# The last layer of 24 chunks as three reduced-precision products per tile in place of one full-precision product

## The reference

```
x = layernorm(x + relu((adj @ x) @ kernel + bias))
u, v = x, v_node_feats
for _ in range(3):
    v = mlp_uv(adj @ u)      # three 128x128 layers, each followed by leaky_relu
    u = mlp_vu(adj @ v)
x = layernorm(x + v)
```

## The kernel before

| rows | chunks | loads at offsets from 12 on |
|---|---|---|
| 1 | 4 | 14 (after a copy of a PSUM bank to `part`, L580), 16, 22, 24 |
| 2 to 5, and 6 in the last of the four passes | 17 | 12, 14, 20, 22 |
| 6 in the other three passes | 3 | 16, 18, 24, 26 |

## Time and profile before

### The profile page before, as it was taken

How to read it: one execution, slowest core, us unless ns; L and a number is a source line. 1 busy time by engine, 2 the same in 40 slices (tenths; PEclk the granted TensorE clock), 3 DMA queues, 4 the chain that set the end, 5 groups by cost and what they waited for, 6 DMA issues and landing times.

```text
span 1169.0 us, 13697 instructions
## 1 busy us (share of the span) xinstructions
PE 1154.0 (99%) x5236; PEld 953.1 (82%) x5236; DVE 738.2 (63%) x890; ACT 660.8 (57%) x809; POOL 0.2 (0%) x4
## 2 busy tenths in 40 slices
PE   7999999999999999999999999999999999999997
PEld 6888888888888888888888888888888888887776
DVE  7997676458564555555545756554566555658886
ACT  7765554346554555555444754554566454557885
POOL 0000000000000000000000000000000000000000
PEclk9999999999999999999999999999999999999999
DMA  9988775568466646555656736655665566569891
GB/s 383 405 299 327 244 270 192 206 215 288 124 207 209 215 161 214 198 185 180 216 180 216 250 118 216 214 173 181 210 222 188 190 205 209 193 217 362 296 323 50
DMA packets 72210, 261.60 MB, mean 224 GB/s; under 512 B 8017, under 2 KB 8657, under 8 KB 71121
## 3 DMA queue, kind: packets, MB, share of 16 engines
q1 hardware_dynamic: 72000, 260.61, 64.2%
q10 hardware_dynamic: 144, 0.13, 0.0%
HBM read 258.61 MB, written 2.10 MB: 223 GB/s over the span
## 4 chain that ended last, share of the span: by engine, by line
PE 92%; DMA 3%; DVE 2%; ACT 2%; issue 1%; SPq 0%; DVEq 0%; ACTq 0%
PE agg_ps L872 28%; PE agg_ps L865 28%; PE agg_ps L858 28%; PE pre_ps L769 4%; DMA adj_raw<-in_adj 3%; PE hid_ps L730 1%; PE hid_ps L732 1%; PE hid_ps L731 1%; DVE adj_lo L722 1%; ACT adj_hi L593 1%; PE hid_ps L791 1%; PE hid_ps L805 0%; DVE stats L606 0%; ACT hid L487 0%; ACT resid L508 0%
## 5 line engine op out<-in xcount | busy, mean ns | idle before, releaser
L722 DVE TENSOR_TENSOR adj_lo<-adj_raw,adj_hi 128x1024 fp32r<-128x1024 f32 x488 | 576.7, 1220 | 230.2 <-ACT adj_hi L593 224.0
L858 PE MATMUL agg_ps<-adj_hi,feat_hi 128*128 128x512 f32 x1532 | 607.7, 397 | 7.4 <-ACT adj_hi L593 7.4
L865 PE MATMUL agg_ps<-adj_hi,feat_lo 128*128 128x512 f32 x1532 | 598.0, 390 | 0.0
L593 ACT ACTIVATE adj_hi<-adj_raw 128x1024 fp32r<-128x1024 f32 x488 | 492.8, 1052 | 94.8 <-PE agg_ps L872 80.3
L872 PE MATMUL agg_ps<-adj_lo,feat_hi 128*128 128x512 f32 x1532 | 473.8, 390 | 0.2 <-DVE adj_lo L722 0.2
L858 PEld LDWEIGHTS agg_ps<-adj_hi,feat_hi 128*128 128x128 f32 x1532 | 288.5, 188 | 68.8 <-issue 10.2
L865 PEld LDWEIGHTS agg_ps<-adj_hi,feat_lo 128*128 128x128 f32 x1532 | 288.5, 188 | 62.2 <-issue 3.4
L872 PEld LDWEIGHTS agg_ps<-adj_lo,feat_hi 128*128 128x128 f32 x1532 | 287.8, 188 | 61.9 <-DVE adj_lo L722 1.5
L487 ACT ACTIVATE hid<-hid_ps,params 128x512 f32<-128x512 f32 (+1 forms) x80 | 54.5, 681 | 59.1 <-PE hid_ps L732 50.6
L558 ACT ACTIVATE in_hi<-part 128x512 fp32r<-128x512 f32 x24 | 15.2, 634 | 110.3 <-DVE part L711 110.3
L487 ACT ACTIVATE post<-pre 128x512 f32<-128x512 f32 x39 | 24.6, 630 | 79.8 <-DVE pre L689 79.8
(11 more groups left out here) (70 smaller groups left out, 262.2 us busy)
## 6 DMA issues: line engine op xcount, KB each, us to landing
adj_raw<-in_adj SPq DMA_DIRECT2D x472, 512.0 KB, 5.7
adj_raw<-in_adj SPq DMA_DIRECT2D x8, 1024.0 KB, 8.1
resid<-in_x SPq DMA_DIRECT2D x8, 256.0 KB, 8.0
out<-resid SPq DMA_DIRECT2D x7, 256.0 KB, 6.8
params<-in_weights SPq DMA_DIRECT2D x1, 386.0 KB, 4.7
b_row<-in_bias_rows SPq DMA_DIRECT2D x1, 128.0 KB, 5.5
out<-resid ACTq DMA_DIRECT2D x1, 128.0 KB, 2.1
out<-resid SPq DMA_DIRECT2D x1, 128.0 KB, 2.2
```

Of the source, the lines that this page charges most:

```text
L593: act.activation(adj_hi[:, plan.slot[b], i * CHUNK:(i + pieces) * CHUNK], adj_raw[:, h % RAW, 0:pieces * CHUNK], ACT.Copy).then_inc(adj_hi ...
L722: dve.tensor_tensor(adj_lo[:, plan.slot[b], slot], adj_raw[:, h % RAW, 0:pieces * CHUNK], adj_hi[:, plan.slot[b], slot].bitcast(F32), ALU. ...
L858: pe.matmul(group_bank(g), feat_hi[feats][:, tile(src, i)], adj_hi[:, plan.slot[b], piece(i)], start=start, stop=False)
L865: pe.matmul(group_bank(g), feat_lo[feats][:, tile(src, i)], adj_hi[:, plan.slot[b], piece(i)], start=False, stop=False)
```

## The change

The last layer (`pe_out`) of the 24 `IN_PARTS` chunks is made in parts. For each of its four tiles three F32R products of 128 x 128 take the place of one full-precision product. ScalarE writes the high part `hid2_hi` from PSUM ahead of `hid2`; VectorE writes `hid2_lo` in a new step `dve_hid2=16`; the last layer's two weights are split once, at tick 320. The steps `pe_out`, `dve_pre`, `act_post` and `dve_feat` move one tick later.

```diff
-                   pe_out=18, dve_pre=19, act_post=20, dve_feat=22),
+                   dve_hid2=16, pe_out=19, dve_pre=20, act_post=21, dve_feat=23),
...
+    def out_in_parts(self, u):
+        return "dve_hid2" in STEPS[self.steps_of(u)]
...
                     act.wait_ge(params_loaded, 32)
                     act.activation(w_hi[:, :, :], w_hid, ACT.Copy).then_inc(w_hi_ready, 1)
+                    act.activation(w_out[:, :, 0:P], w_last, ACT.Copy).then_inc(w_out_hi_ready, 1)
...
+                    if plan.out_in_parts(u):
+                        prelu(hid2_hi[:, :], hid2_ps[:, :], bias=b_col[:, b:b + 1]).then_inc(hid2_hi_ready, 1)
                     prelu(hid2[:, own(u)], layer_bank(1, u), bias=b_col[:, b:b + 1]).then_inc(hid2_ready, 1)
...
+                    dve.wait_ge(w_out_hi_ready, 1)
+                    dve.tensor_tensor(w_out[:, :, P:2 * P], w_last, w_out[:, :, 0:P].bitcast(F32), ALU.subtract)\
+                       .then_inc(w_out_lo_ready, 1)
...
+                u = at(t, "dve_hid2", DEEP)
+                if u is not None:
+                    dve.wait_ge(hid2_hi_ready, plan.count_out_in_parts(u))
+                    dve.wait_ge(hid2_ready, u + 1)
+                    dve.tensor_tensor(hid2_lo[:, :], hid2[:, :], hid2_hi[:, :].bitcast(F32), ALU.subtract)\
+                       .then_inc(hid2_lo_ready, 1)
...
-                    for k, j in enumerate(tiles_of(u)):
+                    if plan.out_in_parts(u):
+                        k = SPLIT_OUT[kind_of(u)]
+                        if plan.count_out_in_parts(u) == 1:
+                            pe.wait_ge(w_out_lo_ready, 1)
+                        pe.wait_ge(hid2_lo_ready, plan.count_out_in_parts(u))
+                        for j in tiles_of(u):
+                            nodes = slice(j * P, (j + 1) * P)
+                            last = product(pre_ps[:, nodes], (hid2_hi[:, nodes], hid2_lo[:, nodes]),
+                                           (w_out[:, k, 0:P], w_out[:, k, P:2 * P]))
+                    for k, j in enumerate(tiles_of(u) if not plan.out_in_parts(u) else ()):
```

More of the change, by code:

```diff
@@ L245, in in_parts, with count_out_in_parts @@
         return self.steps_of(u) in (IN_PARTS, TURN)
+    def out_in_parts(self, u):
+        return "dve_hid2" in STEPS[self.steps_of(u)]
+    def count_out_in_parts(self, u):
+        return sum(self.out_in_parts(i) for i in range(u + 1))
     def count_in_parts(self, u):
@@ L280, in gnn_kernel @@
     OUT_W = {GCN: 0, UV: 5, VU: 6, LAST: 5}
+    SPLIT_OUT = {UV: 0, VU: 1}
     OUT_BIAS = {GCN: 0, UV: 1, VU: 2, LAST: 1}
@@ L303, in gnn_kernel @@
         w_lo = sb("w_lo", [P, N_SPLIT, P], F32R)
+        w_out = sb("w_out", [P, len(SPLIT_OUT), 2 * P], F32R)
         b_row = sb("b_row", [P, N_BIASES * P])
@@ L310, in gnn_kernel @@
         hid2 = sb("hid2", [P, CHUNK])
+        hid2_hi = sb("hid2_hi", [P, CHUNK], F32R)
+        hid2_lo = sb("hid2_lo", [P, CHUNK], F32R)
         pre = sb("pre", [P, CHUNK])
@@ L334, in gnn_kernel @@
         w_lo_ready = sem("w_lo_ready")
+        w_out_hi_ready = sem("w_out_hi_ready")
+        w_out_lo_ready = sem("w_out_lo_ready")
         x_hi_ready = sem("x_hi_ready")
@@ L351, in gnn_kernel @@
         hid2_ready = sem("hid2_ready")
+        hid2_hi_ready = sem("hid2_hi_ready")
+        hid2_lo_ready = sem("hid2_lo_ready")
         pre_done = sem("pre_done")
@@ L368, in gnn_kernel @@
         w_hid = w_raw[:, 1:1 + N_SPLIT, :]
+        w_last = w_raw[:, OUT_W[UV]:OUT_W[VU] + 1, :]
         b_col = params[:, N_WEIGHTS * P:]
```

## The result

| | before | after |
|---|---|---|
| time, median of 5 runs | 1171.18 us (1170.98 to 1171.26) | 1202.67 us (1202.48 to 1203.54) |
| span of the profiled execution | 1169.0 us | 1201.7 us |
| granted TensorE clock | 0.999 | 0.993 |

The ratio of the mean times is 1.0272 (95% interval 1.0261 to 1.0284); by the medians the change is 31.5 us slower, where 28.0 were forecast. The profiled execution is the slowest of the five (1203.54 us); its span grew by 32.7 us.

What follows compares the result with a forecast made beforehand. TensorE, busy 99% of the span, was taken to bound the kernel. Stream 10.7 plus waits 6.6, 0.7 and 10.0 made 28.0 us, so 1171.03 us would become 1199.0 us, range 1181 to 1204.

Steps and rivals of the forecast that it cites:

- The price of a short product: TensorE's last layer: 12 F32R products at 0.112 us take 1.34 us instead of 0.90; 10.7 us over 24 chunks.
- A: Rival for the last layer: price goes by columns, 0.067 us a product, waits stay; 1186.0 us, chance 0.13.
- B: Rival for the last layer: a short F32R product costs as much as a full-precision one; 1231 us, chance 0.08.
- E: Rival for the last layer: load and columns one after the other, 0.16 us a product; 1213 us, chance 0.03.
- The wait for `hid2_lo` in 17 chunks: Rows 2 to 5, once row 6: TensorE waits 0.39 us for `hid2_lo`, behind a load's `adj_lo`; 6.6 us.
- Row 1's own wait for it: Row 1's last layer, 4 chunks: TensorE waits 0.18 us each for `hid2_lo`; 0.7 us.
- The wait for the features at row 1: `feat_lo` falls behind a load's `adj_lo` on VectorE; TensorE waits 2.5 us, 4 times; 10.0 us.
- Rival C: ScalarE and VectorE far enough ahead to hide the waits; only the stream remains; 1181.7 us, chance 0.08.
- D: Rival: TensorE alone counts and goes by columns, no waits; 1168.7 us, 0.2% faster, chance 0.02.
- TensorE's clock: Clock over the whole kernel: granted at 0.999 of its full 2.4 GHz, nothing priced for it.
- The forecast's own case: Likeliest case, stream growth plus all three waits: 1199.0 us, own range 1193 to 1203, chance 0.66.

Runs made afterwards that it cites:

- number 3: Changed kernel with `hid2_lo` written at offset 14 and `pe_out`, `dve_pre`, `act_post`, `dve_feat` back at 18, 19, 20, 22: 1181.40 us.
- number 5: As number 3, but two products a tile, leaving out high part of `hid2` times low part of the weight: 1170.66 us.
- 6: As number 3, but the weight's parts stationary and `hid2`'s parts moving: three products of 512 columns with 3 loads instead of 12 of 128: 1165.68 us.
- number 7: As number 3, but two of each tile's products joined into one of 256 columns: 8 products and loads a layer, same 1536 columns: 1171.71 us.
- 9: As number 5, with the second product left out too: one product a tile, high x high alone: 1160.82 us.
- Number 1: Changed kernel with only `dve_feat` moved from 23 to 22, so `feat_lo` comes ahead of the load's `adj_lo`: 1190.84 us.
- number 4: Kernel before with only `dve_feat` moved from 22 to 23, behind the load's `adj_lo`, no product changed: 1181.36 us.
- number 2: Changed kernel with only `dve_hid2` moved from 16 to 14, ahead of the `adj_lo` of the load due there: 1191.33 us.
- Number 8: As number 2, with six tiles of one first-pass last layer multiplied once more, shifting later work by 1.34 us: 1195.22 us.
- number 10: The changed kernel run again without an edit: 1202.02 us.
- number 11: The changed kernel with six tiles of one first-pass last layer multiplied once more, shifting later work by 1.34 us: 1203.92 us.

## Why the prediction was right, and where it was not

- **The price of a short product** (10.7 us). Right, and for the reason given: 0.112 us in the trace, 10.4 us in number 3. Numbers 5, 6, 7 and 9 show that the number of products, each with its load, is paid for: 4, 8 and 12 of them give 1160.8, 1170.7 and 1181.4 us, while columns come nearly free (number 7). That it is the load and not another cost of each product is not shown by these numbers, since every product here has one load. It rests on the traces: the loads stand 0.11 apart also where nothing else holds them, and where a load was in early the next product followed after 0.06 (435.01 to 435.07). The row that the forecast called the nearest, the full-precision records at 0.112, was a weaker guide than it seemed, because their columns alone come to 0.107 (number 5). The load spacing of the earlier trace rows carries the term. Rivals A, B and E are out.
- **The wait for `hid2_lo` in 17 chunks** (6.6 us). Right in mechanism and in size, 0.39 us each, but only 13 came in the profiled execution, 5.1 us. The other four, those of row 2, were covered by the slow clock.
- **Row 1's own wait for it** (0.7 us). As forecast, 4 times.
- **The wait for the features at row 1** (10.0 us). Right: `feat_lo` complete within 0.05 us of the time worked out, 2.5 us lost each time. Number 1 shows that the order of `feat_lo` and `adj_lo` is the cause, number 4 that it needs nothing else of the change. Rival C, hidden waits, is out with it, and D.
- **TensorE's clock** (nothing). This step failed: "I price nothing for TensorE's clock". In the first profile the four waits brought four stretches at 1.2 GHz, 6.4 us, less the 1.6 of the waits that these covered. That leaves 4.8 us; the miss in the span is 4.7 (32.7 against 28.0). The five runs, at clocks of 0.993 to 0.995, lie at 1202.5 to 1203.5. The forecast's own case adds up to 1171.0 + 13.0 + 6.6 + 0.7 + 10.8 = 1202.1 us at most, and the measured 1202.67 lies above that. That it is still within the range stated, 1181 to 1204, is luck as far as the clock goes: no term of the range allowed for it.
- **What stays open** is when a wait of this length costs the clock. Its length doesn't decide: 2.6 us did and did not, in numbers 2, 8 and 10. Number 8 points to the moment at which it falls, but on another chip and with one slow stretch of four waits, and number 11 adds nothing to it. Why number 2 had a clock of 0.999 in all four of its runs while the changed kernel had 0.993 to 0.996 in all nine is not settled. The two profiles of the changed kernel also differ at the span's start, where products stand 0.43 us apart at first: they come down to 0.23 from about 10.2 us in the first profile and 12.7 in number 10, with the first wait at 304.66 and 304.78. Whether that bears on it was not tested.

## What to carry to other kernels

Count weight loads before columns: with a stationary tile of 128 x 128 and only 128 columns to move, an F32R product cost the same 0.112 us as each of the two records of a full-precision product, so three parts cost 0.34 us against 0.22. With 512 columns to move it was the other way round: three F32R products 0.68 us, two full-precision records 0.86. Splitting a layer into parts paid here only where the moving operand was wide. When a step is moved by one tick, look at what else is due at the tick it lands on, on each engine: here `feat_lo` slipped behind the `adj_lo` of a load whose `adj_hi` ScalarE writes only after `feat_hi`, the step that feeds `feat_lo`. One tick, 0.7 us, became 2.5 us of wait at each of four places that had no slack. A wait of 2.5 us on TensorE is to be priced with its clock, here between nothing and 1.6 us more each.

## What the runs showed of the hardware that was not expected

- Each of the 11 slow stretches of the clock lasted 3.41 us. One began before the wait was over (307.11, 0.15 before the first product behind it), others up to 1.4 us after TensorE had resumed (in number 10 at 507.67, 0.6 after; in number 4 at 503.17, behind a start at 501.74). Within 2.57 to 2.61 us from start to start, the same wait brought one or didn't.
- In the line of products of 128 columns only the first step was short, 0.06 us, behind the one product whose load had run ahead of it. The line through 512 and 256 columns gave 0.067. That the array would keep this lower price if every tile were there in time is likely from this, but no run shows it.
- The Trainium skill, page "TensorE: Matmul & The Clock Gate", section "Back-to-back issue gap", has 81 ns for a pair of load and product at 128 columns. With F32R tiles 112 ns were measured here, in twelve pairs a layer, 24 times; for this kernel the measurement decides.
